# A selective-scan stage whose TensorE products are put in order of array form, with the row's first cumulative sums moved to the top of the turn

## The reference, cut to what matters

```python
dA_cs = jnp.cumsum(dt * A, axis=2)                                   # within a chunk of 128
Lmat = jnp.exp(dA_cs[:, :, :, None, :] - dA_cs[:, :, None, :, :])
att = einsum('bcihn,bcjhn->bcijh', Ch, Bh) * Lmat * dt               # causal part only
y_intra = einsum('bcijh,bcjhp->bcihp', att, xc)
states = einsum('bcjhn,bcjh,bcjhp->bchpn', Bh, decay_to_end * dt, xc)
carry = carry * exp(dA_cs[-1]) + states                              # from row to row
y_inter = einsum('bcihn,bcih,bchpn->bcihp', Ch, jnp.exp(dA_cs), previous_carry)
y = layernorm(y_intra + y_inter + D * x) * norm_w + norm_b
out = (y * z) @ out_proj_w.T                                         # z = in_proj of the row
```

## Time and profile before

| | |
|---|---|
| median of 3 runs | 2518.32 us (2510.87 to 2520.17) |
| the profiled execution | 2516.11 us |
| its span from first to last instruction | 2514.1 us |
| mean granted TensorE clock | 0.955 of full speed |
| TensorE busy, of the span | 2202.5 us (88%) |
| VectorE, ScalarE, GpSimd busy | 66%, 52%, 44% |

### The profile page before, as it was taken

The page is one execution under the profiler, slowest core; times in us unless marked ns, Lnnn a source line. Parts: engine busy times, 40 slices in busy tenths (PEclk is TensorE's granted clock), DMA queues, the critical chain, the costliest instruction groups (busy, mean ns, idle before and its releaser), DMA issues. The chain is left out here.

```text
span 2514.1 us, 64417 instructions
## 1 busy us (share of the span) xinstructions
PE 2202.5 (88%) x23092; PEld 1626.4 (65%) x23092; DVE 1662.3 (66%) x3168; ACT 1304.1 (52%) x2719; POOL 1113.6 (44%) x1393
## 2 busy tenths in 40 slices
PE   0699988997899169999999999999996989969998
PEld 0565636786688137777777777777775756447563
DVE  5345575664565168888888888888883455834557
ACT  0355440174047247777777777777762555424544
POOL 0333250000000137788787787788772232533325
PEclk9999998999899579999999999999998999979999
DMA  8624495415523312222222222222225134961459
GB/s 210 178 79 85 126 316 140 108 34 190 177 51 122 115 35 58 59 61 56 59 60 56 59 60 56 59 60 56 60 49 169 51 77 103 332 182 51 85 125 318
DMA packets 305628, 272.25 MB, mean 108 GB/s; under 512 B 175966, under 2 KB 238846, under 8 KB 299210
## 3 DMA queue, kind: packets, MB, share of 16 engines
q1 hardware_dynamic: 294698, 256.00, 36.7%
q0 software_dynamic: 9280, 6.44, 2.1%
q10 hardware_dynamic: 1496, 7.63, 0.8%
HBM read 165.29 MB, written 81.46 MB: 98 GB/s over the span
## 5 line engine op out<-in xcount | busy, mean ns | idle before, releaser
L1669 DVE TENSOR_TENSOR l_scan_att<-l_scan_decay,l_scan_causal_scores 128x512 f32<-128x512 f32 x384 | 326.7, 851 | 64.3 <-ACT l_scan_decay L1638 64.0
L715 ACT COPY l_arena<-l_body_bank 128x384 f32<-128x384 f32 x192 | 142.0, 901 | 262.3 <-PE l_body_bank L587 262.3
L1632 ACT ACTIVATE l_scan_decay<-l_scan_cum 128x512 f32<-128x512 f32 x384 | 216.2, 597 | 32.7 <-PE l_scan_cum L1524 32.5
L1638 ACT ACTIVATE l_scan_decay<-l_scan_decay 128x512 f32<-128x512 f32 x384 | 227.8, 631 | 4.1
L1649 ACT ACTIVATE l_scan_yw<-l_scan_y_by_channel,l_scan_norm_b,l_scan_norm_w 128x128 f32<-128x128 f32 x384 | 148.0, 456 | 125.4 <-PE l_scan_y_by_channel L1586 124.4
L1571 PE MATMUL l_scan_gate_projected<-l_scan_xr,l_wf 97*128 97x128 f32 (+1 forms) x1536 | 205.3, 283 | 1.3 <-DVE l_scan_xo L1724 1.2
L1602 PE MATMUL l_scan_gate_projected<-l_scan_yz,l_scan_wo 128*96 128x128 f32 x1536 | 198.5, 279 | 1.1 <-DVE l_scan_yz L1701 1.1
L567 POOL TENSOR_TENSOR l_arena<-l_arena 96x512 f32<-96x512 f32 x96 | 122.7, 1279 | 167.8 <-ACT l_arena L780 160.3
L1602 PEld LDWEIGHTS l_scan_gate_projected<-l_scan_yz,l_scan_wo 128*96 128x96 f32 x1536 | 170.9, 163 | 40.0 <-issue 29.6
L1489 POOL TENSOR_TENSOR l_scan_inter<-l_scan_inter,l_scan_xd 128x384 f32<-128x384 f32 x128 | 128.0, 1000 | 150.7 <-DVE l_scan_inter L1684 150.7
L1571 PEld LDWEIGHTS l_scan_gate_projected<-l_scan_xr,l_wf 97*128 97x128 f32 (+1 forms) x1536 | 181.0, 190 | 17.2 <-issue 2.2
(11 more groups left out here) (193 smaller groups left out, 5064.8 us busy)
## 6 DMA issues: line engine op xcount, KB each, us to landing
l_scan_xc<-convolved_rows SPq DMA_DIRECT2D x128, 224.0 KB, 2.8
x_after<-l_arena SPq DMA_DIRECT2D x64, 384.0 KB, 5.0
l_arena<-x_after SPq DMA_DIRECT2D x64, 384.0 KB, 5.7
convolved_rows<-l_slots SPq DMA_DIRECT2D x48, 441.0 KB
l_conv_x_main<-x_after SPq DMA_DIRECT2D x64, 256.0 KB, 2.6
l_arena<-x_after SPq DMA_DIRECT2D x16, 1024.0 KB, 8.6
prepare_xt<-x SPq DMA_DIRECT2D x8, 1536.0 KB
l_arena<-x SPq DMA_DIRECT2D x32, 384.0 KB, 5.7
```

Source lines behind the costliest of these rows:

```text
L715: nc.scalar.copy(tA[:, b, :, j:j + 2].rearrange("p c q -> p q c"), bank[n % 4][:, 0:2 * C].rearrange("p (q c) -> p q c", q=2)).then_inc(t_ ...
L1632: nc.scalar.activation(decay[:, b % 2, 4 * g:4 * g + 4, :], cum[(b + g) % 2][:], ACT.Relu, scale=-1.0)\
L1638: nc.scalar.activation(group, group, ACT.Exp, scale=-1.0).then_inc(exp_done, 1)
L1669: nc.vector.tensor_tensor(att[:, b, 4 * g:4 * g + 4, :], decay[:, b % 2, 4 * g:4 * g + 4, :], causal[:, b % 2:b % 2 + 1, :].broadcast_to([ ...
```

## The change

TensorE's order becomes: cumulative 0, the transpose L1548, L1541, L1594, L1554, L1561, cumulative 1, L1571, L1579, L1586, cumulative 2, L1602. By form: full, 32 columns, 32 partitions, full to the end. L1594 writes the other half of its PSUM bank (`half_s`) and no longer waits for VectorE's L1684 (`scaled`); the wait for the state update of the row before (`state_ready`) now stands ahead of it. ScalarE takes `gaps(0)` first, then B and C, then `y_intra`, and `decays(0)` ahead of `gaps(1)`. VectorE updates the state ahead of `attention(1)`, and adds the residual (`xo`) ahead of `attention(2)`. GpSimd and SyncE are not edited.

```diff
--- before.py
+++ after.py
@@ -1379,7 +1379,7 @@
         p_bcg = ph.ps("bcg", [128, 2, W])
         p_y = ph.ps("y_intra", [128, D_INNER])
         p_i = ph.ps("y_inter", [128, 2, BANK])
-        half_i = slice(0, D_INNER // 2)
+        half_i, half_s = slice(0, D_INNER // 2), slice(D_INNER // 2, D_INNER)
         p_zo = ph.ps("gate_projected", [128, BANK])
         p_z = p_zo[:, 0:3 * W].rearrange("p (m w) -> p m w", w=W)
         p_o = p_zo[0:CH, 0:2 * W].rearrange("p (k w) -> p k w", w=W)
@@ -1528,6 +1528,12 @@
                 def turn(at):
                     row0, row2, row3, row4 = (at(lag) for lag in (0, 2, 3, 4))
 
+                    if row0:
+                        cumulative(row0, 0)
+                        r, b, n = row0
+                        pe.wait_ge(xc_landed[b], n * 32 + 32)
+                        pe.wait_ge(masked, r + 1)
+                        nc.tensor.transpose(p_bcg[:, 0, :], xc[:, b, CONV_DIM + N_STATE - 128:], ident[:]).then_inc(bc_turned, 1)
                     if row2:
                         r, b, n = row2
                         pe.wait_ge(xs_ready, 3 * r + 3)
@@ -1541,25 +1547,21 @@
                                 last = nc.tensor.matmul(p_yt[h * HEAD:(h + 1) * HEAD, g, :], xdt[:, b % 2, head],
                                                         att[:, b, 4 * g + h, :], start=(g == 0), stop=(g == 2))
                         last.then_inc(yi_done, 1)
-                    if row0:
-                        r, b, n = row0
-                        pe.wait_ge(xc_landed[b], n * 32 + 32)
-                        pe.wait_ge(masked, r + 1)
-                        nc.tensor.transpose(p_bcg[:, 0, :], xc[:, b, CONV_DIM + N_STATE - 128:], ident[:]).then_inc(bc_turned, 1)
-                    if row2:
-                        r, b, n = row2
                         pe.wait_ge(state_ready, r + 1)
+                        for g in range(2):
+                            last = nc.tensor.matmul(p_i[g * N_STATE:(g + 1) * N_STATE, 0, half_s], xc[:, b, D_INNER:D_INNER + N_STATE],
+                                                    xw[:, b % 2, g * D_INNER // 2:(g + 1) * D_INNER // 2], start=True, stop=True)
+                        last.then_inc(st_done, 1)
                         for g in range(2):
                             at = slice(g * N_STATE, (g + 1) * N_STATE)
                             last = nc.tensor.matmul(p_i[:, g, half_i], bct[at, b, 1, :], state[at, :], start=True, stop=True)
                         last.then_inc(inter_done, 1)
                     if row0:
-                        cumulative(row0, 0)
-                        cumulative(row0, 1)
                         r, b, n = row0
                         pe.wait_ge(bc_copied, r + 1)
                         nc.tensor.matmul(p_bcg[:, 1, :], bct[0:N_STATE, b, 0, :], bct[0:N_STATE, b, 1, :], start=True, stop=True)\
                             .then_inc(scores, 1)
+                        cumulative(row0, 1)
                     if row4:
                         r, b, n = row4
                         pe.wait_ge(xr_landed[b], n * 16 + 16)
@@ -1587,13 +1589,6 @@
                         last.then_inc(turned, 1)
                     if row0:
                         cumulative(row0, 2)
-                    if row2:
-                        r, b, n = row2
-                        pe.wait_ge(scaled, r + 1)
-                        for g in range(2):
-                            last = nc.tensor.matmul(p_i[g * N_STATE:(g + 1) * N_STATE, 0, half_i], xc[:, b, D_INNER:D_INNER + N_STATE],
-                                                    xw[:, b % 2, g * D_INNER // 2:(g + 1) * D_INNER // 2], start=True, stop=True)
-                        last.then_inc(st_done, 1)
                     if row4:
                         r, b, n = row4
                         pe.wait_ge(yz_done, r + 2)
@@ -1612,34 +1607,36 @@
 
                 def turn(at):
                     row0, row2, row3 = (at(lag) for lag in (0, 2, 3))
+
+                    def gaps(g):
+                        r, b, n = row0
+                        act.wait_ge(cum_done, 3 * r + g + 1)
+                        nc.scalar.activation(decay[:, b % 2, 4 * g:4 * g + 4, :], cum[(b + g) % 2][:], ACT.Relu, scale=-1.0)\
+                            .then_inc(gap_done, 1)
+
+                    def decays(g):
+                        r, b, n = row0
+                        act.wait_ge(gap_done, 2 + 3 * r + g + 1)
+                        group = decay[:, b % 2, 4 * g:4 * g + 4, :]
+                        nc.scalar.activation(group, group, ACT.Exp, scale=-1.0).then_inc(exp_done, 1)
+
+                    if row0:
+                        r, b, n = row0
+                        act.wait_ge(att_done, 3 * r)
+                        gaps(0)
+                        act.wait_ge(bc_turned, r + 1)
+                        if not (isinstance(r, int) and r < U):
+                            act.wait_ge(inter_done, r - 2)
+                        nc.scalar.copy(bct[0:N_STATE, b, 0, :], p_bcg[N_STATE:2 * N_STATE, 0, :])
+                        nc.scalar.copy(bct[:, b, 1, :], p_bcg[2 * N_STATE:4 * N_STATE, 0, :]).then_inc(bc_copied, 1)
                     if row2:
                         r, b, n = row2
                         act.wait_ge(yi_done, r + 2)
                         act.wait_ge(y_back, r)
                         nc.scalar.copy(yt[:], p_yt[:]).then_inc(yt_kept, 1)
                     if row0:
-                        r, b, n = row0
-                        act.wait_ge(bc_turned, r + 1)
-                        if not (isinstance(r, int) and r < U):
-                            act.wait_ge(inter_done, r - 2)
-                        nc.scalar.copy(bct[0:N_STATE, b, 0, :], p_bcg[N_STATE:2 * N_STATE, 0, :])
-                        nc.scalar.copy(bct[:, b, 1, :], p_bcg[2 * N_STATE:4 * N_STATE, 0, :]).then_inc(bc_copied, 1)
-                        act.wait_ge(att_done, 3 * r)
-
-                        def gaps(g):
-
-                            act.wait_ge(cum_done, 3 * r + g + 1)
-                            nc.scalar.activation(decay[:, b % 2, 4 * g:4 * g + 4, :], cum[(b + g) % 2][:], ACT.Relu, scale=-1.0)\
-                                .then_inc(gap_done, 1)
-
-                        def decays(g):
-                            act.wait_ge(gap_done, 2 + 3 * r + g + 1)
-                            group = decay[:, b % 2, 4 * g:4 * g + 4, :]
-                            nc.scalar.activation(group, group, ACT.Exp, scale=-1.0).then_inc(exp_done, 1)
-
-                        gaps(0)
+                        decays(0)
                         gaps(1)
-                        decays(0)
                         decays(1)
                     if row3:
                         r, b, n = row3
@@ -1708,20 +1704,20 @@
                         nc.vector.bn_stats(st6[:, b], y[:, b % 2]).then_inc(counted, 1)
                         hold(dve, counted, r + 1, passed)
                         nc.vector.bn_aggr(mv[:, b], st6[:, b]).then_inc(agg, 1)
+                        dve.wait_ge(st_done, r + 2)
+                        dve.wait_ge(faded_done, r + 1)
+                        nc.vector.tensor_tensor(state[:], p_i[0:2 * N_STATE, 0, half_s], faded[:], ALU.add).then_inc(state_ready, 1)
                     if row0:
                         attention(row0[0], row0[1], 1)
-                    if row2:
-                        r, b, n = row2
-                        dve.wait_ge(st_done, r + 2)
-                        dve.wait_ge(faded_done, r + 1)
-                        nc.vector.tensor_tensor(state[:], p_i[0:2 * N_STATE, 0, half_i], faded[:], ALU.add).then_inc(state_ready, 1)
-                    if row0:
-                        attention(row0[0], row0[1], 2)
                     if row4:
                         r, b, n = row4
                         dve.wait_ge(o_done, r + 1)
                         dve.wait_ge(stored[b], n * 16 + 16)
                         nc.vector.tensor_tensor(xo[:, b], p_o[:], xr[0:CH, b], ALU.add).then_inc(xo_done, 1)
+                    if row0:
+                        attention(row0[0], row0[1], 2)
+                    if row4:
+                        r, b, n = row4
                         dve.wait_ge(xo_done, r + 1)
                         for kk in range(2):
                             nc.vector.bn_stats(stats[:, kk, bass.ds(r, 1), :], xo[:, b, kk, :]).then_inc(stats_done, 1)
```

## The result

The changed kernel takes 2478.77 us (median of 4 runs, 2477.59 to 2485.05) against 2514.6 us before: a ratio of 0.987, 95% interval 0.985 to 0.990. So it is faster, but by less than half of what was forecast (2432), and the time lies just outside the range (2478). The profiled execution's span is 2475.7 us against 2514.1, 38.4 less. One of the ten executions of the control kernel further down took 4056.4 us at a granted clock of 0.795 and is left out of its interval.

The account below looks back on a forecast made before the run. TensorE was taken to bound the scan; its turn would fall from 7.54 to 6.84 us, and 123 turns x 0.70 = 86 us off the profiled 2516.1 gave 2430, 2432 as median. Own range 2422 to 2445, wider range to 2478.

Parts of the forecast that it names:

- What bounds the kernel before, and what a change of form costs: In the scan, TensorE's sequence sets the 7.54 us turn; form changes add drains of about 0.09 and bare first weights.
- the sum: TensorE's new group lengths over one scan turn, added up: 6.84 us, 0.70 less than before.
- No drain between bf16 and float32 in one form: At three full-array boundaries on TensorE, bf16 to float32 costs no drain; otherwise the turn would be about 7.25 us.
- Whether the others keep up at 6.84: Check that ScalarE, VectorE, GpSimd and the input load fit a 6.84 us scan turn, with margins from 0.1 to 1.7.
- The walk: Step through one scan turn from cumulative 0, placing the other engines' work; attention 0 was charged 0.7 us of waiting.
- The 5.78 us that it gave VectorE unhindered: VectorE's need per scan turn without attention collisions: its 6.35 busy us less 3 x (0.861 - 0.67).
- the gaps are not due to form: TensorE's gaps come from waits or type changes: half saved, 2482 us, chance 0.03; nothing saved, 2518 us, chance 0.04.
- VectorE becomes the bound: Two attention products in the scan meet GpSimd operations: 7.16 us a turn, 47 us saved, 2471 us, chance 0.10.
- The transpose late for its input: TensorE's transpose waits for SyncE's load in one row of four: 28 us, giving 2460 us, chance 0.05.
- the slower side: GpSimd blocks all three VectorE attention products: 7.85 us a turn, 38 us lost, 2556 us, chance 0.04.

Follow-up runs that it names:

- the control kernel further down: The kernel before with only VectorE's scaling of y_inter put ahead of its normalisation: 2517.7 us, ratio 1.000.
- The spare products: The change with VectorE's scaling first, plus one 8-column bf16 product ahead of L1581: full stationary 2431.6 us, 32-column stationary 2457.7 us.
- the TensorE-bound kernel: The changed kernel with VectorE's scaling of y_inter put ahead of its normalisation: 2424.1 us, ratio 0.964, 6.77 us a turn.

## Why the prediction was wrong

- **What bounds the kernel before, and what a change of form costs: right.** The spare products show form as the cause, and the TensorE-bound kernel runs TensorE's new order in 6.77 us, where the sum said 6.84. The sum's error was in the bf16 groups: cumulative 0, 1 and 2 take 0.05 to 0.06 less each, as no longer load shows behind them. The gate takes 0.06 more and L1597 0.03 more; the first load of each starts only 0.05 ahead of its product (1204.19 and 1204.24), where L1579's started 0.11 ahead in the kernel before.
- **No drain between bf16 and float32 in one form: right** (cumulative 0 to the transpose in 0.44).
- **Whether the others keep up at 6.84: this is the step that failed.** The walk followed VectorE and TensorE with margins of 0.1 and 0.3 and gave GpSimd one line, that its idle before L1489 "is where the shorter turn comes out of". It put the wait of the normalisation for GpSimd's L1507 at nothing and charged it no collision (0.46 before). The runs showed in its place: the normalisation waits 0.14 a turn for L1507, which ends 0.43 behind attention 2, and then meets the fade and takes 0.82. These two terms are 0.43 of the 0.45 us by which the turn of 7.22 misses TensorE's 6.77. The scaling stands behind the normalisation in VectorE's queue, L1489 and attention 0 behind the scaling, and `yz` behind attention 0, so the delay reaches TensorE.
- On VectorE the walk also missed 0.07 in attention 1 and two short idle stretches of each turn: 0.14 between the mask and attention 0, which waits for the mask to finish, and 0.16 between the statistics L1708 and their aggregate L1710. The 5.78 us that it gave VectorE unhindered has neither of these stretches in it.
- **The rivals.** By number the nearest was "the gaps are not due to form" with half the gain, 7.25 a turn and 2482 us, at a chance of 0.03; that is luck, since the spare products contradict its mechanism. By mechanism the nearest was "VectorE becomes the bound", 7.16 a turn and 2471 us, at a chance of 0.10. But what came was not a second blocked attention product: it was one blocked attention, a blocked normalisation and the wait for GpSimd's power. Its price for one collision (0.69) held, 1.39 - 0.67 = 0.72.
- **The transpose late for its input, and the slower side:** neither was seen; no wait for the input stands in the view of waits.
- **The range** ended at 2478 because it summed two waits of attention products as the worst plausible; a chain that closes over two engines was in none of the cases.
- The prediction took VectorE's and ScalarE's edits as a package to match. They are not equal: with neither, TensorE's order loses 1.4%; with ScalarE's alone it gains 1.3%, as much as with both. TensorE's order with VectorE's alone was not run.

The version that beats both is the change with VectorE's scaling ahead of its normalisation: 2424.1 us, 3.6% under before and 2.2% under the change.

## What to carry to other kernels

Before crediting a saving to the engine that is full, follow each idle stretch of the others back through its releasers; if the chain comes home to the same engine a turn later, its length can bound the turn though no engine in it is always busy (here VectorE 95%, GpSimd 87%). In an in-order queue, put the instruction that others wait for ahead of the one that waits for others: behind the reordering that one exchange was worth 54.7 us, and in the kernel before nothing. And a change of array form between small products is paid in time, so grouping them pays, once the orders of the engines that feed them are moved with them.

## What the runs showed of the hardware that was not expected

VectorE's normalisation is a tensor_scalar with one tensor input from SBUF and two per-partition scalars. It took 0.46 us before, 0.82 where it started 0.1 us ahead of GpSimd's fade, and 0.52 when the fade was cut to 16 columns. So an instruction with one tensor input can be held up by GpSimd too; attention, with two, was the only one suspected. GpSimd's short copy L1478, which runs at the same moment, was not varied.

GpSimd's power on a single column took 0.57 us in some turns and 1.12 to 1.20 in others. Where it is long it ends 0.43 us after the end of the attention product that started 0.02 to 0.09 us behind it, so the collision costs the short instruction about the length of the long one. It does not happen each time: in the kernel with the spare 32-column product the power starts the same 0.09 us ahead of attention 2 as after the change and takes 0.57 in every turn. What decides that is not shown.
